# A decoder layer with routed experts: the experts' second layer from the 25th block on as f32r products of high and low parts

## The chip, the cores and the metric

One core of a Trainium2 chip runs the whole program. The metric is the device time of one execution in microseconds, from the hardware. Lower is better. The traces come from one profiled execution.

## The reference

Input x is 4 x 1024 x 256 in f32, a context is 4 x 77 x 256. Three stages follow, each on a layer norm of x and added to x:

```python
x = x + self_attention(layernorm(x))        # 16 heads of 16, a bias that falls with distance
x = x + cross_attention(layernorm(x), ctx)
x = x + ffn(layernorm(x))

def ffn(x):                                  # 8 experts, the best 2 per token
    logits = flat_x @ W_router + b_router
    top_vals, top_idx = top_k(logits, 2)
    router_weights = softmax(logits of the two, -inf elsewhere)
    for e in range(8):
        h = relu(flat_x @ W1[e] + b1[e])     # 256 -> 1024
        y = h @ W2[e] + b2[e]                # 1024 -> 256
        out += y * router_weights[:, e]
```

## The kernel before, in words

The kernel has two phases. In the first, some 1120 us, it computes the attention of four batches. Beside it, the tokens of finished batches are layer-normed and routed, and each token's row (256 values, its number, a code of its expert and two weights) is scattered by GpSimd into a DRAM array `expert_rows` that has one region for each expert.

The second phase goes through 71 blocks (`NBLK`) of 128 rows, all of one expert each. A small table, computed on the chip, says which expert (`expert_of`) and which rows (`row_of`) a block has; it is made in two parts, for blocks below `EARLY` = 40 before the last batch is done and for the others after. The order of all steps on all engines is written out by one planner, `plan()`: it appends steps to one list, with estimated costs in `TAKES`, and each engine later goes through the whole list and does its own kinds of step in that order. Semaphores tie the engines together. `blocks()` (L450) emits for block n:

- `load` (SP): weights of the first layer of block n+3, 1 MB, into one of three buffers `w1_now`; then the block's 128 rows, 130 KB, into one of `NX` = 4 buffers `xi`. SP waits at L990 for the first layer of block n (which frees the buffer of weights), and at L994 for the landed scatter-add of the block that used the same `xi`.
- `up` (TensorE, L1231): first layer of block n+1, in two halves of four chunks of 128 hidden columns, each chunk two f32 products with the rows as the moving side (128 columns). The output is transposed, with hidden units on the partitions. ScalarE (`hid_fore`, L1378) and VectorE (`hid_aft`, L1654) add the bias, take the positive part and write `hidT`, two buffers.
- `xi_turn` (TensorE, L1219) and `xi_turned` (ScalarE, L1364): two transposes of the rows of block n+2.
- `down` (TensorE, L1254): second layer of block n. Eight f32 products add into one PSUM bank; each has a chunk of `hidT` as the stationary side and 256 columns of `w2` as the moving side. All of W2 (8 MB) has been in SBUF since the end of attention; the expert's number is read into a register of TensorE's queue (L1248) first. From block 40 on two banks alternate.
- `yo` (VectorE, L1664 to L1669): the weight of each row from its code, two small chained operations, the bias times this weight, and the sum times the weight out of PSUM into `yo`, two buffers. It waits for the landed scatter-add of block n-2.
- `added` (GpSimd, L1753): an indirect DMA that adds the 128 rows of `yo` into the output in DRAM. L1752 makes it wait until the scatter-add of block n-1 has landed, since two could touch one token.

In the trace an f32 product on TensorE shows as two records, each with its own weight load; so `up` has 32 records for each block and `down` 16.

## Time and profile before

| what | us |
|---|---|
| median of 3 runs (lowest, highest) | 1685.94 (1683.2, 1687.22) |
| the profiled execution's own time | 1687.17 |
| its span, first to last instruction | 1685.3 |
| TensorE busy (matmul) | 1616.5 (96%) |
| VectorE busy | 1026.2 (61%) |
| ScalarE busy | 786.4 (47%) |
| GpSimd busy | 321.8 (19%) |
| mean granted clock of TensorE | 0.986 of full speed |

"Busy" of TensorE is modelled: its records overlap, so that the time from the start of one to the start of the next is what counts, not the duration of one. Idle time of an engine is told with what ended it ("<-"); a wait for several semaphores is put down to one of them. "SPq", "DVEq" or "POOLq" is an engine's instruction queue. The expert phase begins at about 1116 us of the span.

### The profile page before, as it was taken

How to read it: one execution, taken by the hardware profiler on the slowest of the kernel's cores; microseconds unless marked ns; L12 is line 12 of the kernel's file. 1: busy time of each engine (PE TensorE's matmuls, PEld its weight loads, DVE VectorE, ACT ScalarE, POOL GpSimd, SP SyncE). 2: the span in 40 equal slices, each digit the busy share in tenths (PEclk: the TensorE clock that was granted, in tenths of full speed). 3: DMA queues.
4: the chain of work that ended last, by engine and by line, in shares of the span. 5: the costliest groups of instructions: out<-in, count | busy, mean ns of one | idle time of the engine just before them, and what ended most of it. 6: DMA issues, size and time to landing. Idle time of an engine off the chain costs nothing.

```text
span 1685.3 us, 29721 instructions
## 1 busy us (share of the span) xinstructions
PE 1616.5 (96%) x10022; PEld 964.5 (57%) x10022; DVE 1026.2 (61%) x2366; ACT 786.4 (47%) x1635; POOL 321.8 (19%) x310
## 2 busy tenths in 40 slices
PE   5999999999999999999999999989999999999996
PEld 2333334344454444444434453369998899899996
DVE  4888887888777778877788775333444233323322
ACT  3046655666546766655675657742221122121221
POOL 6101120001200041210031100332252222122121
PEclk9789999999999999999999999999999999999998
DMA  6820440333241440323422612235566665656653
GB/s 172 155 70 29 101 80 9 34 42 55 50 70 35 73 80 8 42 60 83 67 56 39 141 49 104 111 107 161 152 199 188 188 188 164 182 168 180 185 163 74
DMA packets 92661, 173.30 MB, mean 103 GB/s; under 512 B 13236, under 2 KB 51124, under 8 KB 92385
## 3 DMA queue, kind: packets, MB, share of 16 engines
q1 hardware_dynamic: 75376, 143.69, 34.0%
q0 software_dynamic: 15744, 26.54, 7.4%
q8 instruction: 82, 1.34, 0.4%
q10 hardware_dynamic: 1392, 1.18, 0.3%
q14 instruction: 67, 0.54, 0.1%
HBM read 133.69 MB, written 37.29 MB: 101 GB/s over the span
## 4 chain that ended last, share of the span: by engine, by line
PE 88%; DVE 3%; ACT 3%; DMA 3%; issue 2%; ACTq 0%; POOL 0%; SPq 0%; POOLq 0%; DVEq 0%
PE ps L1039 15%; PE ps L1254 14%; PE ps L1231 14%; PE ps L1065 14%; PE ps L1025 13%; PE ps L1095 3%; DVE rmax L1409 2%; ACT prob L1272 2%; PE ps L1117 2%; PE ps L1104 2%; PE ps L1151 2%; PE ps L1086 2%; PE ps L1028 2%; PE ps L1068 2%; DMA out<-yo,xi 1%
## 5 line engine op out<-in xcount | busy, mean ns | idle before, releaser
L1409 DVE TENSOR_REDUCE rmax<-ps 128x1 f32<-128x512 f32 x1024 | 665.9, 686 | 198.1 <-PE ps L1065 96.3
L1272 ACT ACTIVATE prob<-ps 128x512 f32<-128x512 f32 x1024 | 560.7, 600 | 331.6 <-PE ps L1028 178.4
L1065 PE MATMUL ps<-stacked_k,stacked_q 112*128 112x512 bf16 x1024 | 397.6, 392 | 10.7 <-DVE rmax L1409 6.3
L1025 PE MATMUL ps<-stacked_q,stacked_k 115*128 115x512 bf16 x1024 | 361.6, 383 | 7.2 <-ACT prob L1272 4.9
L1039 PE MATMUL ps<-prob,values 128*32 128x512 f32 x2048 | 273.5, 606 | 5.6 <-ACT prob L1272 5.6
L1231 PEld LDWEIGHTS ps<-xiT,w_now 128*128 128x128 f32 x2272 | 265.3, 192 | 3.5
L1231 PE MATMUL ps<-xiT,w_now 128*128 128x128 f32 x2272 | 267.1, 275 | 0.0
L1254 PE MATMUL ps<-w,hidT 128*128 x1136 | 259.9, 382 | 6.9 <-issue 5.9
L1065 PEld LDWEIGHTS ps<-stacked_k,stacked_q 112*128 112x128 bf16 x1024 | 100.5, 98 | 285.4 <-DVE rmax L1409 209.9
L1378 ACT ACTIVATE hidT<-ps,b 128x128 f32<-128x128 f32 x284 | 81.1, 368 | 352.8 <-PE ps L1231 315.0
L1254 PEld LDWEIGHTS ps<-w,hidT 128*128 128x128 f32 x1136 | 210.2, 190 | 39.7 <-issue 13.6
L1654 DVE TENSOR_SCALAR hidT<-ps,b 128x128 f32<-128x128 f32 x284 | 80.2, 345 | 201.4 <-PE ps L1231 196.9
L1025 PEld LDWEIGHTS ps<-stacked_q,stacked_k 115*128 115x128 bf16 x1024 | 98.5, 99 | 168.4 <-ACT prob L1272 87.2
L1753 POOL DMA_INDIRECT out<-yo,xi x71 | 111.0, 1563 | 415.4 <-DVE yo L1669 403.2
L1028 PE MATMUL ps<-ramps,slopes 128*128 128x128 f16 x512 | 113.2, 221 | 0.0
L1068 PE MATMUL ps<-ramps,slopes 128*128 128x128 f16 x512 | 113.2, 221 | 0.0
L1669 DVE SCALAR_TENSOR_TENSOR yo<-ps,weight,bias 128x256 f32<-128x256 f32 x71 | 34.3, 484 | 118.8 <-PE ps L1254 118.7
L1739 POOL DMA_INDIRECT expert_rows<-xn,slot x64 | 62.1, 970 | 159.1 <-ACT prob L1272 105.4
L1687 POOL TENSOR_TENSOR rstd_of<-varp,minus_half 128x8 f32<-128x8 f32 (+1 forms) x14 | 21.5, 1533 | 368.6 <-DVE varp L1457 368.6
L1039 PEld LDWEIGHTS ps<-prob,values 128*32 128x32 f32 x2048 | 40.3, 108 | 76.9 <-issue 49.5
L1095 PE MATMUL ps<-xT_next,wqkv 128*128 128x512 f32 x128 | 68.1, 631 | 4.4 <-DVE rest_of L1480 3.2
L1068 PEld LDWEIGHTS ps<-ramps,slopes 128*128 128x128 f16 x512 | 50.5, 99 | 23.1 <-issue 5.4
(181 smaller groups left out, 1128.2 us busy)
## 6 DMA issues: line engine op xcount, KB each, us to landing
w_now<-in_w SPq DMA_DIRECT2D x71, 1024.0 KB
stacked_q<-parts_of_rows SPq DMA_DIRECT2D x90, 128.0 KB, 6.0
stacked_k<-parts_of_rows SPq DMA_DIRECT2D x90, 128.0 KB, 6.6
xi<-expert_rows SPq DMA_DIRECT2D x71, 130.0 KB
w<-in_w SPq DMA_DIRECT2D x8, 1024.0 KB
parts_of_rows<-q_part SPq DMA_DIRECT2D x21, 256.0 KB, 8.7
parts_of_rows<-k_part SPq DMA_DIRECT2D x21, 256.0 KB, 8.8
xr<-in_x POOLq DMA_DIRECT2D x4, 1024.0 KB, 9.6
```

The lines of the kernel that those rows point to most:

```text
L1025: m = e.matmul(ps[:, bank, :], ka[i][0:ROWS, hh, kt * P:(kt + 1) * P], qa[i][0:ROWS, hh, ch * BANK:(ch + 1) * BANK], start=True, stop=True)
L1028: m = e.matmul(ps[:, bank, (kt % 4) * P:(kt % 4 + 1) * P], slopes[:, g * HG + hh, :], ramps[:, kt % 2, :], start=False, stop=True, skip_gr ...
L1039: m = e.matmul(ps[CT * hh:CT * (hh + 1), AV_BANK, :], vt[b % 2][:, kt, c0:c0 + CT], prob[:, unit_of(G, ch, kt, hh) % NPROB, :], start=(kt ...
L1065: m = e.matmul(ps[:, bank, :], qa[i][0:MAX_ROW, hh, qt * P:(qt + 1) * P], ka[i][0:MAX_ROW, hh, kc * BANK:(kc + 1) * BANK], start=True, sto ...
L1068: m = e.matmul(ps[:, bank, (qt % 4) * P:(qt % 4 + 1) * P], slopes[:, g * HG + hh, :], ramps[:, 1 - qt % 2, :], start=False, stop=True, ski ...
L1095: m = e.matmul(ps[:, bank, :], wqkv[:, part, a * D + mo * P:a * D + (mo + 1) * P], xT_next[:, part, ch * BANK:(ch + 1) * BANK], start=firs ...
L1231: m = e.matmul(ps[:, 1 + 2 * (n % 2) + half, q * P:(q + 1) * P], w1_now[n % NW][:, c, f * P:(f + 1) * P], xiT[n % 2][:, c, :], start=(c == ...
L1254: m = e.matmul(ps[:, down_bank(n), 0:D], hidT[n % 2][:, c, :], w2[:, bass.ds(expert, 1), c, :].rearrange("p a f -> p (a f)"), start=(c == ...
L1272: e.activation(prob[:, u % NPROB, :], ps[:, u % NSCORE, :], ACT.Exp).then_inc(sem["exp"], 1)
L1378: m = e.activation(hidT[n % 2][:, q, :], ps[:, 1 + 2 * (n % 2), q * P:(q + 1) * P], ACT.Relu, bias=b1[:, bass.ds(expert, 1), q])
L1409: e.tensor_reduce(rmax[:, G % 2, hh * NT + qt, kc:kc + 1], ps[:, p.bank("max", *k), :], AX.X, ALU.max).then_inc(sem["maxed"], 1)
L1753: e.indirect_dma_start(t["out"], bass.IndirectOffsetOnAxis(ap=xi[n % NX][:, TOKEN:TOKEN + 1].bitcast(I32), axis=0), yo[n % NY][:, :], None ...
```

## The change

From block `FINE` = 24 on, the second layer is computed from two parts of each operand. ScalarE copies the 128x2048 of W2 that the block needs to a high part in the type f32r (`w2_high`), VectorE subtracts it from the original for the low part (`w2_low`), in one instruction, and both keep three buffers. `hidT` is split in the same way in halves (`hid_high` by ScalarE, `hid_low` by VectorE), with two buffers. TensorE then does three f32r products a chunk (high x high, high x low, low x high), 24 a block. Reading the expert's number leaves TensorE's queue for these blocks. Two PSUM banks alternate from block 24 on. The weights of rows move from VectorE to GpSimd for these blocks, as three operations. SP loads a block's rows ahead of its first-layer weights, with five buffers for rows instead of four, in all blocks. An unused tile, `spare`, goes.

```diff
-NX, NY, NW = 4, 2, 3
+NX, NY, NW = 5, 2, 3
+FINE = 24
+NPARTS = 3
@@ plan(), blocks()
+    def split_rows(n, half):
+        add("hid_high", n, half)
+        add("hid_low", n, half)
                 for half in range(2):
                     up_half(n + 1, half)
+                    if n + 1 >= FINE and half == 0:
+                        split_rows(n + 1, 0)
                     yield
             if n + 2 < NBLK:
                 turn_block(n + 2)
+            if FINE <= n + NPARTS - 1 < NBLK and n + 1 > FINE:
+                add("w2_low", n + NPARTS - 1)
+            if FINE <= n + 1 < NBLK:
+                split_rows(n + 1, 1)
+            if n >= FINE:
+                add("yo_weight", n)
             add("down", n)
             add("yo", n)
             add("added", n)
+            if FINE <= n + NPARTS < NBLK:
+                add("w2_high", n + NPARTS)
+                if n + NPARTS < FINE + 2:
+                    add("w2_low", n + NPARTS)
@@ SP
+                    if n >= NX:
+                        e.wait_ge(sem["added"], 16 * (n - NX + 1))
+                    at = e.value_load(row_of[0:1, n:n + 1], ...)
+                    e.dma_start(xi[n % NX][:, :], rows_in[bass.ds(at, P), :]).then_inc(...)
                     if n >= NW:
                         e.wait_ge(sem["up"], p.upto("up", n - NW, 1))
                     if n >= 2:
                         first_layer(n)
-                    (the wait and the rows' DMA stood here)
@@ TensorE
+            def down_in_parts(n, bank):
+                m = n - FINE
+                e.wait_ge(sem["w2_low"], m + 1)
+                for c in range(FC):
+                    if c % (FC // 2) == 0:
+                        e.wait_ge(sem["hid_low"], 2 * m + 1 + c // (FC // 2))
+                    products = ((hid_high, w2_high), (hid_high, w2_low), (hid_low, w2_high))
+                    for i, (rows, weights) in enumerate(products):
+                        last = e.matmul(ps[:, bank, 0:D], rows[n % 2][:, c, :], weights[n % NPARTS][:, c, :],
+                                        start=(c == 0 and i == 0), stop=(c == FC - 1 and i == 2))
+                last.then_inc(sem["down"], 1)
@@ ScalarE
+                elif kind == "hid_high":
+                    e.wait_ge(sem[("hid_fore", "hid_aft")[half]], n + 1)
+                    e.activation(hid_high[n % 2][:, chunks, :], hidT[n % 2][:, chunks, :], ACT.Copy).then_inc(sem["hid_high"], 1)
+                elif kind == "w2_high":
+                    if n >= FINE + NPARTS:
+                        e.wait_ge(sem["down"], n - NPARTS + 1)
+                    expert = e.value_load(expert_of[0:1, n:n + 1], min_val=0, max_val=NE - 1)
+                    e.activation(w2_high[n % NPARTS][:, :, :], second_layer(expert, slice(0, FC)), ACT.Copy).then_inc(...)
@@ VectorE
+                elif kind == "hid_low":
+                    e.wait_ge(sem["hid_high"], p.upto("hid_high", n, half))
+                    if half == 0 and n >= FINE + 2:
+                        e.wait_ge(sem["down"], n - 1)
+                    e.tensor_tensor(hid_low[n % 2][:, chunks, :], hidT[n % 2][:, chunks, :], hid_high[...].bitcast(F32), ALU.subtract)
+                elif kind == "w2_low":
+                    e.wait_ge(sem["w2_high"], p.upto("w2_high", n))
+                    e.tensor_tensor(w2_low[n % NPARTS][:, chunks, :], second_layer(expert, chunks), w2_high[...].bitcast(F32), ALU.subtract)
@@ GpSimd
+                elif kind == "yo_weight":
+                    if n == FINE:
+                        e.wait_ge(sem["yo"], n)
+                    elif n >= FINE + NY:
+                        e.wait_ge(sem["yo"], n - NY + 1)
+                    weigh(e, n, then).then_inc(sem["yo_weight"], 1)
...
```

`weigh` waits for the block's rows and does `is_equal`, `mult`, `add` on 128x1 values, chained by a semaphore. At block 24 ScalarE's first `hid_high` and `w2_high` also wait for all scatters of rows and all stores of attention's output.

## Rows read from the trace of the kernel before

**Rows 1.** Windows: stretch, busy us (count) by engine, clock, DMA share, GB/s.
```profile
1100.00:1150.00 50.00, 45.68 (x312) 37.31 (x309) 15.41 (x55) 20.18 (x48) 17.08 (x20) 1.00 0.40 123
...
1400.00:1450.00 50.00, 49.37 (x340) 46.11 (x339) 15.87 (x55) 10.66 (x35) 10.87 (x7) 1.00 0.63 178
...
1650.00:1690.00 40.00, 22.31 (x137) 19.94 (x135) 8.47 (x28) 3.05 (x10) 6.22 (x4) 0.86 0.25 46
```
**Rows 2.** Chain of waits about one block: start us, us on the chain.
```profile
1406.36 3.57 PE ps L1231 x32
1409.93 0.22 PE ps L1219 x2
1410.15 3.46 PE ps L1254 x16
```
**Rows 3.** All scatter-adds of 1300 to 1660: duration ns min/median/max, first, last start.
```profile
L1753 POOL DMA_INDIRECT out<-yo,xi x48: 1555/1555/1573, 1300.5 to 1655.5; - x48
```
**Rows 4.** Chain of waits in 1324 to 1349, from block 24's scatter-add.
```profile
1331.51 7.41 DMA out<-yo,xi
...
1339.66 6.63 DMA out<-yo,xi
...
1347.04 3.24 DMA xi<-expert_rows
```
**Rows 5.** Waits of SP's queue, 1400 to 1650: total us, times, longest.
```profile
SPq L995 <- DMA out<-yo,xi: 175.1, 33, 6.3
```
**Rows 6.** Timeline of GpSimd, 1482 to 1545: start us, us, [idle before].
```profile
1482.54 1.55 POOL L1753 DMA_INDIRECT out<-yo,xi  x1 [5.45 <-DVE yo L1669]
...
1520.67 1.55 POOL L1753 DMA_INDIRECT out<-yo,xi  x1 [6.08 <-DVE yo L1669]
1528.32 1.56 POOL L1753 DMA_INDIRECT out<-yo,xi  x1 [6.09 <-DVE yo L1669]
1535.98 1.55 POOL L1753 DMA_INDIRECT out<-yo,xi  x1 [6.11 <-DVE yo L1669]
```
**Rows 7.** Timeline of SP's queue in the same stretch.
```profile
1490.40 0.34 SPq L996 DMA_DIRECT2D xi<-expert_rows  x1
...
1521.92 0.24 SPq L865 DMA_DIRECT2D w_now<-in_w  x1
1528.21 0.34 SPq L996 DMA_DIRECT2D xi<-expert_rows  x1
1529.64 0.40 SPq L865 DMA_DIRECT2D w_now<-in_w  x1
1533.29 0.34 SPq L996 DMA_DIRECT2D xi<-expert_rows  x1
...
1541.79 0.34 SPq L996 DMA_DIRECT2D xi<-expert_rows  x1
```
**Rows 8.** Chain of waits in 1655 to 1690, the last two scatter-adds.
```profile
1669.97 3.74 DMA out<-yo,xi
...
1674.46 1.55 POOL out L1753
```
**Rows 9.** Chain of waits in 1436 to 1465, between transposes and second layer.
```profile
1446.77 0.50 issue
```
**Rows 10.** Groups by form, ScalarE and VectorE: busy us, mean ns, idle before.
```profile
L1272 ACT ACTIVATE prob<-ps 128x512 f32<-128x512 f32 x1024 | 560.7, 600 | 331.6 <-PE ps L1028 178.4 <-PE ps L1025 151.9 <-issue 0.6
L1290 ACT ACTIVATE xn<-xr,shift_of,rstd_of 128x256 f32<-128x256 f32 x64 | 37.6, 604 | 0.8 <-DVE shift_of L1463 0.8
L1364 ACT ACTIVATE xiT<-ps 128x256 f32<-128x256 f32 x71 | 27.2, 383 | 59.0 <-PE ps L1219 59.0
...
L1606 DVE TENSOR_TENSOR more_than<-count,steps 128x256 f32<-128x256 f32 x2 | 0.8, 420 | 0.0
L1545 DVE TENSOR_TENSOR chosen<-first,pick_order 128x32 f32<-128x32 f32 x4 | 0.8, 192 | 0.1
```
**Rows 11.** Durations of the bias operation of yo, ns min/median/max.
```profile
L1667 DVE TENSOR_SCALAR bias<-b_all,weight x71: 352/353/611, 1129.5 to 1670.5; 128x256 f32 x71
```

More of the change, by code:

```diff
@@ L79 @@
     "act": {"exp": 0.61, "av": 0.61, "turned": 0.61, "high": 0.7, "norm": 0.55, "cross_exp": 0.9, "p_turned": 0.55, "weigh_exp": 0.35,
-            "c_turned": 0.45, "kv_made": 0.5, "qk_made": 0.5, "cb_made": 0.4, "cv_made": 0.45, "xi_turned": 0.4, "hid_fore": 1.5},
+            "c_turned": 0.45, "kv_made": 0.5, "qk_made": 0.5, "cb_made": 0.4, "cv_made": 0.45, "xi_turned": 0.4, "hid_fore": 1.5,
+            "hid_high": 0.6, "w2_high": 1.95},
     "dve": {"maxed": 0.67, "nmax": 0.3, "nrow": 1.7, "on": 0.75, "stats": 0.42, "aggr": 0.9, "shift": 0.25, "rest": 0.78, "values": 0.9,
             "add1": 0.72, "add2": 0.72, "cross_max": 1.0, "cross_norm": 1.9, "logits_made": 1.8, "second": 1.2, "weigh": 0.2,
-            "chosen": 0.25, "ranked": 2.0, "slots": 1.7, "rows": 1.4, "table": 1.0, "hid_aft": 1.4, "yo": 1.2},
-    "pool": {"rstd": 1.75, "mid": 0.63, "low": 1.2, "bias1": 0.7, "bias2": 0.7, "scatter": 1.3, "added": 1.6, "fetch": 0.9},
+            "chosen": 0.25, "ranked": 2.0, "slots": 1.7, "rows": 1.4, "table": 1.0, "hid_aft": 1.4, "yo": 1.2, "hid_low": 0.65, "w2_low": 2.35},
+    "pool": {"rstd": 1.75, "mid": 0.63, "low": 1.2, "bias1": 0.7, "bias2": 0.7, "scatter": 1.3, "added": 1.6, "fetch": 0.9, "yo_weight": 0.4},
 }
@@ L805, in build @@
             bias = [sb(f"bias{i}", [P, D]) for i in range(NY)]
+            w2_high, w2_low = ([sb(f"w2_{n}{i}", [P, FC, D], F32R) for i in range(NPARTS)] for n in ("high", "low"))
+            hid_high, hid_low = ([sb(f"hid_{n}{i}", [P, FC, P], F32R) for i in range(2)] for n in ("high", "low"))
         flat = lambda ap: ap.rearrange("p a n -> p (a n)")
@@ L1244, in _ @@
                     else:
[L1245 to L1256 removed]
+                        e.wait_ge(sem["yo"], n if n < FINE else n - 1)
+                    if n >= FINE:
+                        down_in_parts(n, down_bank(n))
+                    else:
+                        if n == 0:
+                            e.wait_ge(sem["table"], p.upto("table", 0, TABLE_PARTS - 1))
+                        expert = e.value_load(expert_of[0:1, n:n + 1], min_val=0, max_val=NE - 1)
+                        for c in range(FC):
+                            if c == 0:
+                                e.wait_ge(sem["hid_fore"], n + 1)
+                            elif c == FC // 2:
+                                e.wait_ge(sem["hid_aft"], n + 1)
+                            m = e.matmul(ps[:, down_bank(n), 0:D], hidT[n % 2][:, c, :], w2[:, bass.ds(expert, 1), c, :].rearrange("p a f -> p (a f)"),
+                                         start=(c == 0), stop=(c == FC - 1))
+                        m.then_inc(sem["down"], 1)
         @block.scalar
@@ L1379, in _, with weigh @@
                     m.then_inc(sem["hid_fore"], 1)
+                elif kind == "hid_high":
+                    n, half = k
+                    chunks = slice(half * FC // 2, (half + 1) * FC // 2)
+                    if half == 0 and n == FINE:
+                        e.wait_ge(sem["scattered"], n_scatters(NB - 1))
+                        e.wait_ge(sem["stored"], 16 * (NB + 1))
+                    e.wait_ge(sem[("hid_fore", "hid_aft")[half]], n + 1)
+                    e.activation(hid_high[n % 2][:, chunks, :], hidT[n % 2][:, chunks, :], ACT.Copy).then_inc(sem["hid_high"], 1)
+                elif kind == "w2_high":
+                    n, = k
+                    if n == FINE:
+                        e.wait_ge(sem["scattered"], n_scatters(NB - 1))
+                        e.wait_ge(sem["stored"], 16 * (NB + 1))
+                    elif n == EARLY:
+                        e.wait_ge(sem["table"], p.upto("table", 1, TABLE_PARTS - 1))
+                    if n >= FINE + NPARTS:
+                        e.wait_ge(sem["down"], n - NPARTS + 1)
+                    expert = e.value_load(expert_of[0:1, n:n + 1], min_val=0, max_val=NE - 1)
+                    e.activation(w2_high[n % NPARTS][:, :, :], second_layer(expert, slice(0, FC)), ACT.Copy).then_inc(sem["w2_high"], 1)
+        def weigh(e, n, then):
+            w, x = weight[n % NY], xi[n % NX]
+            e.wait_ge(sem[f"slots_in{n % NX}"], 16 * (n // NX + 1))
+            if n < FINE:
+                then(e.scalar_tensor_tensor(out=w[:, :], in0=x[:, CODE:CODE + 1], scalar=code_of[:, n:n + 1], in1=x[:, MORE:MORE + 1],
+                                            op0=ALU.is_equal, op1=ALU.mult))
+            else:
+                then(e.tensor_scalar(w[:, :], x[:, CODE:CODE + 1], code_of[:, n:n + 1], None, ALU.is_equal))
+                then(e.tensor_tensor(w[:, :], w[:, :], x[:, MORE:MORE + 1], ALU.mult))
+            return e.tensor_tensor(w[:, :], w[:, :], x[:, SECOND:SECOND + 1], ALU.add)
         def split_rest(e, kind, b, mo, a, ch):
@@ L1673, in _, with then @@
         def _(e):
+            links = [0]
+            def then(ins):
+                links[0] += 1
+                ins.then_inc(sem["pool_chain"], 1)
+                e.wait_ge(sem["pool_chain"], links[0])
             for i in range(NSET):
```

51 lines of the change are left out of this document (26 added, 25 removed).

## The prediction

> **What bounds the kernel now.** I read the windows first, then the chain of waits of single blocks, then the queues by time. In the windows of the expert phase TensorE is busy nearly all the time at the full clock, VectorE and ScalarE under a third, and the DMA engines about 0.6 [rows 1]. In the chain a block has 32 records of the first layer and 16 of the second; one that waits for nothing takes 3.57 + 0.22 + 3.46 = 7.25 us of TensorE [rows 2].
>
> The blocks do not run at 7.25. The scatter-adds into the output, one per block, give the beat: 48 of them between 1300.5 and 1655.5, so 355.0 / 47 = 7.55 us [rows 3]. The reader should see in the chain what the missing 0.3 us is: from block 24 on it goes through a scatter-add's DMA of 7.41 us, the next one's 6.63 us, and then SP's read of a block's rows, 3.24 us [rows 4]. Two loops stand behind it.
>
> Loop 1, scatter to scatter: L1752 lets a scatter start only when the one before has landed. From landing (1331.51 + 7.41) to the next start (1339.66) are 0.74 us [rows 4]. SP waits for the same landing before it fetches rows (5.3 us in each of 33 blocks [rows 5]), and issues them at the same offset, so SP's issue at L996 marks the turnaround in the queue's timeline: the scatter of 1482.54 is followed by the issue at 1490.40 (7.86 us), that of 1520.67 by 1528.21 (7.54), that of 1528.32 by 1533.29 (4.97) [rows 6, 7]. Of the eight pairs from 1482.54 to the last, 1535.98 and 1541.79, six lie between 7.33 and 7.86 and two at 4.97 and 5.81; the mean is 6.99. The page books GpSimd's idle time on VectorE's yo; yet in five of the eight the next scatter starts within 0.11 us of SP's issue (1528.21 and 1528.32), so the landing decides it as much as yo does.
>
> Why so long? The 1 MB weight load is issued 1.1 to 1.4 us after the rows, by the same SP wait. When it comes 1.25 us after the scatter (1521.92) the turnaround is 7.54; at 1.32 (1529.64) it is 4.97 [rows 6, 7]; with no load left, the landing takes 3.74 [rows 8]. So the two transfers race, and a few hundredths of a us decide.
>
> Loop 2, the rows' ring of four: landing of scatter k, rows k+4 (3.24 us above), TensorE's transposes, the expert's number read by TensorE's queue, second layer, yo, scatter. It shows as 0.50 us of "issue" ahead of the second layer [rows 9], in most blocks after the 20th.
>
> **The change, part by part.** *Products.* Per block 16 records at 3.46 / 16 = 0.216 us go, 24 f32r products of 256 columns come. No row shows f32r. Bounds: a record with four-byte weights and 256 column-passes paces at 3.57 / 32 = 0.112, and a transpose, 128 columns with such weights, at 0.22 / 2 = 0.11 [rows 2]: half the columns save nothing, so the weight load alone seems to cost about that, and less is not in sight. The other end is 0.216, the record of the old layer. I take 0.112, the nearest row where 256 columns pass once: 24 x 0.112 = 2.69, and the block's TensorE work is 3.79 + 2.69 = 6.48, against 7.25. The ends are 6.4 and 8.97.
>
> By the Trainium skill (FP8 and Floating Point Precision, TensorE Precision Notes) true f32 takes four passes and the reduced form is read once and cut to 22 bits; by that the sum would be the 6.48 above. No trace here shows it.
>
> *ScalarE.* Per block it gains two copies of 128x512 and one of 128x2048, all from SBUF. Slope from PSUM rows: (600 - 383) / 256 = 0.85 ns an element; 128x256 from SBUF takes 604 [rows 10]. So 0.60 to 0.82 each and 1.9 to 2.13. By the same slope hid_fore's four pieces of 128x128 are 1.1; with the 0.38 of xi_turned it works 4.6 to 5.3 of a block. *VectorE.* From 128x256 in 420 ns and 128x32 in 192 [rows 10]: 1.02 ns an element, so 0.69 twice and 2.27, and hid_aft's four pieces are 1.2; with yo and its bias (about 0.4 each) about 5.7 a block.
>
> These sit on a loop: w2_high(n+3) waits for down(n), because of three buffers, and hid_fore(n+2) is queued behind it. After down(n): value_load and copy 2.9, hid_fore 1.2, hid_high 0.75, hid_low 0.7, hid_aft 1.15, w2_low 2.3, hid_low 0.75, down(n+2) 2.75: 12.5 for two blocks, or 6.3 to 6.6 each. About TensorE's own 6.48; it costs nothing as long as the beat is above that.
>
> *Weights of rows on GpSimd.* Three 128x1 operations a block, put between two scatters, where GpSimd is idle 5.4 us and more [rows 6]. Their result is due 4 us later. Zero; if the cover went, up to 1.5 us.
>
> *Rows ahead of weights, ring of five.* SP's cycle keeps its order (wait, rows, weights), so the race of loop 1 stays. Loop 2 gets one block more and stops binding: from landing k to scatter k+3 are 0.75, the rows' 3.2, VectorE's hid_aft, w2_low, hid_low and yo 5.1, a hop of 0.3, and some 6.7 to land: 16 over three blocks, 5.4 each. The read of the expert's number goes from TensorE's queue.
>
> *What is late next.* Loop 1 alone, which no edit touches. TensorE at 6.5 runs ahead until a load of rows or weights stops it, which SP issues behind the landings, at the same beat. Then yo is always early and every scatter starts 0.74 after the landing before it. Taking the mixture of before, between the 6.99 of the eight pairs and the 7.52 of the six slow ones, I set 7.20 a block.
>
> **The sum.** Blocks 24 to 67: scatters at 1331.51 [rows 4] and 1655.5 [rows 3], 43 steps of 7.53; 43 x 0.33 = 14. The last three steps, 19.0 us to 1674.46 [rows 8]: with no load beside them, three of 3.74 + 0.74 make 13.4, so 5.6. Blocks 16 to 24 without loop 2: about 2. Attention, some two thirds of the span, is untouched. Together 22 us from the profiled 1687.2: 1665. The median of the runs shown is 1.2 lower, which I leave in the range.
>
> TensorE will idle some 0.7 us in each block. The clock should hold: in 1100 to 1150 it idled 4.3 of 50 us at 1.00, and fell to 0.86 only where it idled 18 of 40 [rows 1].
>
> **Rivals.** *TensorE becomes the bound again:* the race at 1.25 against 1.32 us tips to the short turnaround, 5 us, and the block runs at 6.5. 43 x 1.03 + 5.6 + 2 = 52, so 1635. For it: a few hundredths decide, and other code stands around them. Against: only a quarter of the turns were won, and with a shorter block the load comes nearer the scatter.
>
> *The race is always lost:* 7.52 a block, 43 x 0.01 + 5.6 + 2 = 8, so 1679.
>
> *f32r paces like the old record,* 0.216: the block takes 8.97 and the kernel 43 x 1.44 + about 3 = 65 more, 1752. It decides from (7.53 - 3.79) / 24 = 0.156 us a product. For it: the operands are four bytes, as in the record that paces at 0.216. Against: that record passes its columns twice.
>
> *VectorE holds GpSimd.* The last bias operation takes 611 ns instead of 353, beside a scatter's preparation on GpSimd, 1669.97 to 1671.52 [rows 8, 11]: they share something. w2_low would hold the preparation by up to 2.3 us where they meet, inside loop 1. Met in every third block, that is 0.7 a block: 7.9, so 43 x 0.37 = 16 less the 8 of the other steps, 1695; met always, far more. It decides from 0.5 us a block. Against: the 48 scatters took 1.555 to 1.573 [rows 3].
>
> The Trainium skill (GPSIMD Engine Reference, Specifications) says that GpSimd's SBUF interfaces are shared with VectorE, with contention from instructions with two SBUF inputs, which w2_low and hid_low are and the old block's bulk was not; the 611 ns agree that there is contention.
>
> **How the numbers follow.** Forecast 0.45, own range 1655 to 1676; TensorE bound, or on the way there, 0.2; race lost 0.13; f32r slow 0.09; VectorE in the way 0.08; nothing measurable 0.05. A measurement of this kernel tells 0.2% (3.4 us) from no change. Faster 0.77, same 0.08, slower 0.15. The range from 1638 to 1690 leaves out 0.1 at each end.
>
> **What would show it.** L1254's successor with 24 records a block at about 0.11 us; the second layer in 2.7 us; no "issue" ahead of it; scatters 7.2 us apart with SP's rows issued at the same time as each; VectorE over 70% busy. A beat of 6.5 would mean the race was won. A beat above 7.6 would make me wrong: then either the products pace over 0.156 or the scatter's preparation is longer than 1.55.

## The result: slower by 0.3%, and outside the forecast range

The kernel after takes 1691.88 us (median of 20 runs, 1684.26 to 1705.3), the kernel before beside it 1687.29 us (20 runs, 1683.2 to 1691.08). The ratio is 1.0029, 95% interval [1.0018, 1.004]. The profiled execution of after took 1695.34 us, with a span of 1693.5 us and a mean clock of 0.982. That is 8 us more than the profiled 1687.2 us of before; 1665 us were forecast.

### The profile page after: what moved, and what is told of

Read it like the earlier page. It is cut to its first block, busy times and chain, and to the rows that moved or that the text cites. A ratio compares the mean times of both kernels' runs of the same rounds, so it can differ in the third digit from the quotient of the medians.

```text
span 1693.5 us, 30735 instructions
## 1 busy us (share of the span) xinstructions
PE 1594.4 (94%) x10398; PEld 960.5 (57%) x10398; DVE 1169.1 (69%) x2413; ACT 932.8 (55%) x1776; POOL 381.1 (23%) x451
## 4 chain that ended last, share of the span: by engine, by line
PE 69%; DMA 21%; DVE 3%; issue 3%; ACT 3%; ACTq 0%; POOL 0%; SPq 0%; POOLq 0%; DVEq 0%
DMA out<-yo,xi 20%; PE ps L1080 15%; PE ps L1106 14%; PE ps L1066 13%; PE ps L1272 5%; PE ps L1298 4%; PE ps L1136 3%; DVE rmax L1486 2%; ACT prob L1316 2%; PE ps L1158 2%; PE ps L1145 2%; PE ps L1192 2%; PE ps L1109 2%; PE ps L1127 2%; PE ps L1069 2%
## 5 line engine op out<-in xcount | busy, mean ns | idle before, releaser
L1272 PE MATMUL ps<-xiT,w_now 128*128 128x128 f32 x2272 | 271.5, 277 | 32.8 <-issue 32.8
L1864 POOL DMA_INDIRECT out<-yo,xi x71 | 128.8, 1813 | 356.9 <-DMA out<-yo,xi 244.3
L1432 ACT ACTIVATE hid_high<-hidT 128x512 fp32r<-128x512 f32 x94 | 59.3, 631 | 96.0 <-DVE hidT L1731 94.5
L1037 PE MATMUL ps<-w_high,hid_high 128*128 128x256 f32 x376 | 110.1, 293 | 0.0
L1748 DVE TENSOR_TENSOR w_low<-w,w_high 128x2048 fp32r<-128x2048 f32 x47 | 107.8, 2293 | 2.4 <-issue 1.9
L1037 PE MATMUL ps<-w_low,hid_high 128*128 128x256 f32 x376 | 106.2, 283 | 0.0
L1037 PE MATMUL ps<-w_high,hid_low 128*128 128x256 f32 x376 | 106.1, 282 | 0.0
L1444 ACT ACTIVATE w_high<-w 128x2048 fp32r x47 | 89.9, 1912 | 22.0 <-PE ps L1037 12.9
```

The costliest lines, as they stand in the source:

```text
L1037: last = e.matmul(ps[:, bank, 0:D], rows[n % 2][:, c, :], weights[n % NPARTS][:, c, :], start=(c == 0 and i == 0), stop=(c == FC - 1 and i ...
L1272: m = e.matmul(ps[:, 1 + 2 * (n % 2) + half, q * P:(q + 1) * P], w1_now[n % NW][:, c, f * P:(f + 1) * P], xiT[n % 2][:, c, :], start=(c == ...
L1444: e.activation(w2_high[n % NPARTS][:, :, :], second_layer(expert, slice(0, FC)), ACT.Copy).then_inc(sem["w2_high"], 1)
L1748: e.tensor_tensor(w2_low[n % NPARTS][:, chunks, :], second_layer(expert, chunks), w2_high[n % NPARTS][:, chunks, :].bitcast(F32), ALU.subt ...
L1864: e.indirect_dma_start(t["out"], bass.IndirectOffsetOnAxis(ap=xi[n % NX][:, TOKEN:TOKEN + 1].bitcast(I32), axis=0), yo[n % NY][:, :], None ...
```

## The profile after, read against the rows of before

From the page of after: the scatter-add's group and the groups of the new second layer (busy us, mean ns of one, idle time ahead and what ended it).

```profile
L1864 POOL DMA_INDIRECT out<-yo,xi x71 | 128.8, 1813 | 356.9 <-DMA out<-yo,xi 244.3
L1432 ACT ACTIVATE hid_high<-hidT 128x512 fp32r<-128x512 f32 x94 | 59.3, 631 | 96.0 <-DVE hidT L1731 94.5
L1037 PE MATMUL ps<-w_high,hid_high 128*128 128x256 f32 x376 | 110.1, 293 | 0.0
```

The groups by form hold the rest.

```profile
L1748 DVE TENSOR_TENSOR w_low<-w,w_high 128x2048 fp32r<-128x2048 f32 x47 | 107.8, 2293 | 2.4 <-issue 1.9
L1444 ACT ACTIVATE w_high<-w 128x2048 fp32r x47 | 89.9, 1912 | 22.0 <-PE ps L1037 12.9 <-issue 9.0
L1740 DVE TENSOR_TENSOR hid_low<-hidT,hid_high 128x512 fp32r<-128x512 f32 x94 | 64.4, 685 | 10.0 <-ACT hid_high L1432 9.7
L1760 DVE TENSOR_SCALAR bias<-b_all,weight 128x256 f32 x71 | 25.2, 354 | 104.2 <-POOL weight L1456 100.1 <-DVE weight L1456 4.1
```

The work of each engine is what the forecast said: 2293 ns for 2.27, 685 for 0.69, 1912 for 1.9 to 2.13, 631 for 0.60 to 0.82. One row is not: the scatter-add's record on GpSimd, its preparation, takes 1813 ns in the mean, where before every one took 1555 to 1573 [rows 3]. This is all scatters of 1300 to 1660 in after, with their duration (min/median/max, first and last start) and the time from the start to the landing of the data.

```profile
L1864 POOL DMA_INDIRECT out<-yo,xi x46: 1553/1797/3065, 1299.0 to 1653.2; - x46
...
DMA to landing us min/median/max: 4.3/7.0/8.4
```

They come every 354.2 / 45 = 7.87 us, against 7.55 [rows 3]. The windows of after answer to [rows 1].

```profile
1100.00:1150.00 50.00, 45.67 (x311) 37.12 (x308) 15.55 (x56) 20.39 (x48) 17.28 (x20) 1.00 0.43 133
1400.00:1450.00 50.00, 43.57 (x367) 42.37 (x365) 36.39 (x62) 28.93 (x50) 14.78 (x24) 1.00 0.63 180
```

TensorE is busy 43.57 of 50 us, where before it was 49.37, at the same full clock; VectorE went from 15.87 to 36.39. TensorE has the time that its shorter block gives, and spends it waiting. The chain of waits, where before it went through both loops [rows 4], is now one loop only.

```profile
1498.36 7.08 DMA out<-yo,xi
1505.44 0.03 issue
1505.46 0.02 POOLq L1863
1505.48 0.50 issue
1505.98 0.02 POOLq L1449
1506.00 0.19 issue
1506.19 7.28 DMA out<-yo,xi
...
1514.23 6.91 DMA out<-yo,xi
```

Landing, 0.75 us, scatter, landing: loop 1 of the forecast. A scatter starts within 0.8 us of the landing before it in 40 of the 42 steps between blocks 24 and 66; in before it did in 15. The waits of the stretch 1400 to 1650 say the same (total us, times, longest): GpSimd waits for the landing 31 times, where before the page booked its idle time on yo.

```profile
POOL out L1864 <- DMA out<-yo,xi: 152.7, 31, 6.5
DVE bias L1760 <- POOL weight L1456: 74.0, 33, 3.9
```

So the step that failed is inside this loop. The timelines of VectorE and of GpSimd in one stretch (start us, us, idle before) show a first part of it.

```profile
1456.45 2.29 DVE L1748 TENSOR_TENSOR w_low<-w,w_high 128x2048 fp32r<-128x2048 f32 x1
...
1464.61 2.29 DVE L1748 TENSOR_TENSOR w_low<-w,w_high 128x2048 fp32r<-128x2048 f32 x1
...
1471.91 2.29 DVE L1748 TENSOR_TENSOR w_low<-w,w_high 128x2048 fp32r<-128x2048 f32 x1
```

```profile
1458.47 1.76 POOL L1864 DMA_INDIRECT out<-yo,xi  x1 [5.00 <-DMA out<-yo,xi]
1459.71 0.87 POOL L1454 TENSOR_SCALAR weight<-xi,code_of 128x1 f32<-128x1 f32 x1
...
1466.29 2.08 POOL L1864 DMA_INDIRECT out<-yo,xi  x1 [5.17 <-DMA out<-yo,xi]
...
1473.80 1.88 POOL L1864 DMA_INDIRECT out<-yo,xi  x1 [4.54 <-DMA out<-yo,xi]
```

Add the end of each w_low and 1.47 us: 1458.74 + 1.47 = 1460.21, and the scatter's preparation ends at 1460.23; 1466.90 gives 1468.37, it ends at 1468.37; 1474.20 gives 1475.67, it ends at 1475.68. The preparation is held by the w_low that runs when it starts, and ends 1.47 us behind it. hid_low holds it in the same way. From block 24 on, 31 of 47 preparations are longer than 1.65 us, up to 3065 ns, and each ends 1.46 to 1.50 us behind such an instruction: 17 behind a w_low, 14 behind a hid_low. The mean is 1.90 us. That is 0.35 us a block, while the landing became later by 1.0 us (mean of blocks 24 to 65: 7.09 against 6.10). The rest has to be found by experiments.

Where the 8 us are, from the scatters' starts in the two traces: up to block 24, 1.1 less; blocks 24 to 67, 338.3 us against 324.0, 14.2 more; the last three steps, 14.2 against 18.9, 4.7 less.

## The experiments

Theory A: VectorE's instructions with two inputs from on-chip memory hold the scatter's preparation. Theory B: the race of scatter and weight load alone, tipped by moved timing. Theory C, formed later: GpSimd's own small instructions behind a scatter hold it. All runs are summed up here; times are medians, ratios are to the kernel before, run beside each. Beat (scatter to scatter) and landing (start to landing) are means over the 42 steps between blocks 24 and 66, preparation over blocks 24 to 70, all of the one profiled execution, so they can differ from the median's tendency: kernels bound by the landing vary by 3 to 21 us from run to run.

| kernel | us | ratio, 95% interval | beat | landing | preparation |
|---|---|---|---|---|---|
| before | 1687.29 | 1 | 7.53 | 6.10 | 1.56 |
| after | 1691.88 | 1.0029 [1.0018, 1.004] | 7.87 | 7.09 | 1.90 |
| ring_alone | 1673.33 | 0.9903 [0.9875, 0.9931] | 7.24 | 6.45 | 1.56 |
| no_w2_low | 1685.3 | 0.9964 [0.9944, 0.9983] | 7.76 | 6.98 | 1.64 |
| two_outputs | 1643.09 | 0.9721 [0.9704, 0.9738] | 6.69 | 5.45 | 1.65 |
| load_behind_prep | 1646.49 | 0.9734 [0.9713, 0.9755] | 6.62 | 4.51 | 1.69 |
| weights_on_dve | 1681.84 | 0.9984 [0.9967, 1.0001] | 7.38 | 6.60 | 2.04 |
| low_behind_prep | 1688.37 | 1.0029 [1.0011, 1.0048] | 7.76 | 6.81 | 1.63 |
| ring_two_input | 1688.35 | 1.003 [1.0018, 1.0041] | 7.60 | 6.81 | 2.89 |
| ring_one_input | 1674.28 | 0.9944 [0.9927, 0.9961] | 7.32 | 6.53 | 1.56 |
| ring_gpsimd_weights | 1675.62 | 0.995 [0.9932, 0.9969] | 7.43 | 6.65 | 1.60 |
| no_w2_low_weights_on_dve | 1679.44 | 0.9967 [0.995, 0.9985] | 7.39 | 6.53 | 1.57 |
| gate_all | 1642.32 | 0.9754 [0.9734, 0.9773] | 6.68 | 3.98 | 1.68 |
| gate_all_f32 | 1668.76 | 0.9911 [0.9892, 0.9929] | 7.24 | 3.83 | 1.57 |
| products_alone | 1671.65 | 0.9909 [0.9891, 0.9927] | 7.42 | 6.64 | 1.56 |
| splits_alone | 1682.56 | 0.9972 [0.9955, 0.999] | 7.67 | 6.89 | 2.08 |
| products_w2_high | 1678.95 | 0.9953 [0.9939, 0.9968] | 7.50 | 6.72 | 1.56 |
| products_hid_split | 1676.41 | 0.9942 [0.9926, 0.9958] | 7.38 | 6.60 | 1.59 |

### First four: which part, and which loop

**ring_alone**: the kernel before with the two queue edits.

```diff
-NX, NY, NW = 4, 2, 3
+NX, NY, NW = 5, 2, 3
 (and SP issues a block's rows ahead of its weight load, as in the change)
```

> The kernel before with only the order of SP's loads and the ring of five rows' buffers changed. Theory A (the scatter-add's preparation on GpSimd is held by VectorE's two-input instructions; nothing of that is here): preparation stays 1.555 us, the 'issue' ahead of the second layer goes, the beat falls from 7.53 to 7.2 to 7.5 us a block, 1668 to 1682 us. Theory B (once every scatter-add starts right behind the landing before it, it loses the race with the weight load each time, without any help of VectorE): the beat is 7.5 to 7.8 and the time 1683 or more.

Measured 0.9903: B in its form "1683 or more" is refuted, A holds so far. Still 37 of the 42 landings take over 6 us. The two edits alone gain 16 us. All edits that were meant to speed the products up make it 21 us worse (1.0029 - 0.9903 = 0.0126).

**no_w2_low**: after, the low part of W2 left out; the second product reads the high part.

```diff
-e.tensor_tensor(w2_low[...], second_layer(expert, chunks), w2_high[...].bitcast(F32), ALU.subtract)
-products = ((hid_high, w2_high), (hid_high, w2_low), (hid_low, w2_high))
+products = ((hid_high, w2_high), (hid_high, w2_high), (hid_low, w2_high))
```

> The changed kernel without VectorE's w2_low; the product that read it reads w2_high again, so TensorE's work is the same (the low part of W2 is left out of the result). Theory A: most preparations fall from 1.8 us to 1.56 to 1.65, a few held by hid_low up to 2.1, more races are won, beat 7.2 to 7.5 instead of 7.8, 1668 to 1680 us. Theory B: the beat stays at 7.7 to 7.9, 1688 to 1695 us.

Half of the loss comes back (0.0065), less than A gave and more than B: the preparation is nearly short again (1.64) and the landing still takes 6.98 us. There is a second cause.

**two_outputs**: after, odd blocks are added to a second array, so that a scatter waits for the last but one. The final sum of the two arrays is left out, and each batch is stored twice.

```diff
-e.wait_ge(sem["added"], 16 * n)
-e.indirect_dma_start(t["out"], ...)
+e.wait_ge(sem[f"added{n % 2}"], 16 * (n // 2))
+e.indirect_dma_start((t["out"], out2)[n % 2], ...)
```

> The changed kernel, with the scatter-adds of odd blocks going to a second array in DRAM, so that each waits for the landing of the one before the last (the final sum of the two arrays is left out, and each finished batch is stored twice). Both theories: the serial wait is the only bound, so the beat falls to that of TensorE or of the ScalarE-VectorE loop, 6.6 to 6.9 us, and the time to 1640 to 1655 us. If another loop (weights, rows) binds close behind, the beat stays above 7.3 and the time above 1670.

**load_behind_prep**: after; from block 28 on, SP holds each weight load until GpSimd has the scatter beside it prepared, and issues it ahead of the rows.

```diff
+if n >= FINE + 4:
+    e.wait_ge(sem["up"], p.upto("up", n - NW, 1))
+    e.wait_ge(sem["yo_weight"], n - 4 - FINE + 1)
+    first_layer(n)
```

> The changed kernel, with SP's load of first-layer weights from block 28 on ahead of the rows, and waiting for GpSimd's yo_weight of block n-4, which is queued behind the scatter-add of block n-5, instead of following that scatter-add's landing. Both theories: the load comes after the preparation, the race is always won, landings fall from 7.0 to 3.8 to 4.5 us, the beat to 6.6 to 6.9, the time to 1638 to 1652 us. If the landings stay near 7 us, the weight load beside them was not what makes them long; time 1685 or more.

Both take the chain of landings apart, each in its own way, and both come to the TensorE-bound beat: 6.6 to 6.7 us. In load_behind_prep the race is mostly won: 29 of 42 landings take under 5 us, and TensorE never idles in this window.

```profile
1400.00:1450.00 50.00, 50.00 (x438) 50.00 (x438) 41.77 (x68) 33.80 (x58) 21.03 (x29) 1.00 0.67 189
```

The traces also tell what decides the race. The prediction compared the starts of the load's issue, 1.25 and 1.32 us behind the scatter. The ends are farther apart, and they lie on two sides of the end of the scatter's preparation [rows 6, 7]. The issue of 1521.92 ends at 1522.16, 0.06 us before the preparation does (1520.67 + 1.55 = 1522.22), and the race is lost; that of 1529.64 ends at 1530.04, 0.16 us after it (1528.32 + 1.56 = 1529.88), and the race is won. It is so throughout, between blocks 24 and 66 of the fourteen traces in which nothing holds the load (two_outputs left aside), wherever a load is issued beside a scatter. Where the issue ended before the preparation or less than 0.1 us after it, none of 530 landings took under 5 us. Where it ended later, 45 of 48 did. In ring_alone it ends 0.08 us too early in the median. A longer preparation can thus turn a won race into a lost one, and one edit does little more than that (ring_two_input, below).

### Second four: the preparation

**weights_on_dve**: after, the rows' weights made by VectorE again (two instructions ahead of the bias, as in before).

```diff
-if n < FINE:
-    then(weigh(e, n, then))
-else:
-    e.wait_ge(sem["yo_weight"], n - FINE + 1)
+then(weigh(e, n, then))
```

> The changed kernel, with the weights of rows back on VectorE. So far: ring_alone beats at 7.28 us a block with preparations of 1.556 us, the changed kernel at 7.80 with 1.90, and its scatter-adds' first packets come 5.5 us after their start instead of 4.2. Theory A1 (VectorE's work of a block is released by GpSimd's weights, which stand behind the scatter-add, takes 5.7 us and so ends in w2_low or hid_low just where GpSimd prepares the next one): the preparations fall to 1.56 to 1.65 us in most blocks, beat 7.2 to 7.4, 1667 to 1676 us. Theory A2 (VectorE's two-input work is in the way wherever it stands): preparations 1.8 or more, time 1686 or more. Theory C (GpSimd's own operations behind the scatter-add delay its descriptors, no_w2_low's 4.45 us): first packets at 4.2 us instead of 4.45 to 5.5.

**low_behind_prep**: after; w2_low waits until the scatter beside it is prepared.

```diff
+if n - 2 >= FINE:
+    e.wait_ge(sem["yo_weight"], n - 2 - FINE + 1)
 e.tensor_tensor(w2_low ...
```

> The changed kernel, with w2_low waiting for yo_weight, that is until the preparation of the scatter-add ahead of it is over. Theory A1: VectorE's order stays the same and so does the release, so w2_low moves little; the preparations stay at 1.75 to 1.95 us, the time within 5 us of 1690. Theory A2: w2_low now never meets a preparation, those of 2.6 to 3.1 us go, the mean falls under 1.8 and the time by 3 to 10 us.

Neither came out by any of the theories. weights_on_dve has longer preparations than after, 2.04, and is faster, 0.9984; low_behind_prep has them at 1.63 and gains nothing, 1.0029.

**ring_two_input** and **ring_one_input**: ring_alone with one unused VectorE instruction of 2.29 us right behind each landing.

```diff
+e.tensor_tensor(extra[:, :, :], w2[:, 0, :, :], w2[:, 1, :, :], ALU.subtract)   # two_input
+e.tensor_reduce(extra[:, :, 0], w2[:, 0, :, :], AX.X, ALU.max)                  # one_input
```

> ring_alone (the kernel before with the new order of loads and five rows' buffers) with one more VectorE instruction a block from the 25th, which subtracts one 128x2048 f32 tile from another in SBUF, ahead of yo and right behind the landing that the next scatter-add waits for as well. The sum is used for nothing. Theory A: GpSimd's preparation is held until it ends, 1.55 -> 2.5 to 3.0 us, the race is always lost, beat 7.28 -> 7.6 to 8.3, 1685 to 1715 us. Theory B (no tie between VectorE and the preparation): 1.556 us and 1670 to 1677 us as in ring_alone.

> The same place, with a reduction over one 128x2048 f32 tile in SBUF instead, about as long (2.2 to 2.3 us) but with one input. Theory A in the form that two inputs matter: preparations 1.555 us, beat 7.2 to 7.4, 1668 to 1678 us. If any VectorE work on SBUF holds GpSimd: as ring_two_input.

This pair is the proof of A. The timelines of ring_two_input, first VectorE, then GpSimd:

```profile
1448.55 2.29 DVE L1665 TENSOR_TENSOR extra<-w 128x2048 f32<-128x2048 f32 x1 [2.56 <-DMA out<-yo,xi]
...
1451.32 0.55 DVE L1669 TENSOR_SCALAR bias<-b_all,weight 128x256 f32 x1 [0.15 <-DVE weight L1668]
...
1456.20 2.29 DVE L1665 TENSOR_TENSOR extra<-w 128x2048 f32<-128x2048 f32 x1 [2.32 <-DMA out<-yo,xi]
```

```profile
1449.23 3.04 POOL L1755 DMA_INDIRECT out<-yo,xi  x1 [4.92 <-DMA out<-yo,xi]
1456.86 3.07 POOL L1755 DMA_INDIRECT out<-yo,xi  x1 [4.59 <-DMA out<-yo,xi]
```

And ring_one_input, the same two engines:

```profile
1455.96 2.29 DVE L1665 TENSOR_REDUCE extra<-w 128x8 f32<-128x2048 f32 x1
...
1463.58 2.29 DVE L1665 TENSOR_REDUCE extra<-w 128x8 f32<-128x2048 f32 x1 [0.37 <-DMA out<-yo,xi]
```

```profile
1455.73 1.56 POOL L1755 DMA_INDIRECT out<-yo,xi  x1 [5.96 <-DMA out<-yo,xi]
1464.16 1.56 POOL L1755 DMA_INDIRECT out<-yo,xi  x1 [6.87 <-DMA out<-yo,xi]
```

Same length, same place in the queue. With two inputs the preparation ends 1.4 us behind the VectorE instruction (1450.84, 1452.27), in 42 of the 43 blocks in which that runs when the scatter starts. With one it takes its 1.56 right through it, in all 23 such blocks; the second pair of lines is one. The pair differs in the output too, 128x2048 against 128x8. Writing alone holds nothing in what these traces have, which is shorter instructions: in ring_alone eight `hidT` and seven `bias` operations, which write 128x128 and 128x256 values to on-chip memory, run on for 0.19 to 0.34 us past a scatter's start, and its preparation still takes 1.56 to 1.57.

The two-input instruction costs 14 us over the other (1688.35 against 1674.28), and it does so by the race alone: no short landing is left (0 of 42 under 5 us, against 4), while the long ones take 6.81 us in the mean as against 6.80, though they are prepared 1.3 us later. Against ring_alone, run at another time, the one-input instruction may itself cost up to some us (0.9944 against 0.9903, intervals overlapping).

The Trainium skill (SBUF — State Buffer, Who interferes with whom) infers that tensor_tensor, which takes only the read interface shared with GpSimd, does not stall descriptor generation. This pair shows that it does stall that of a scatter-add with an index tile, by 1.5 us a piece; on tensor_reduce, which by the page never contends, the two agree.

But A is not the whole: low_behind_prep has the preparation repaired and gains nothing, and weights_on_dve, with a longer one, is 0.0045 faster than after. What weights_on_dve takes away is GpSimd's three instructions behind each scatter: hence theory C.

### Third four: GpSimd's own instructions, and the way out

**ring_gpsimd_weights**: ring_alone, the rows' weights on GpSimd from block 24 on.

```diff
-then(e.scalar_tensor_tensor(out=w[:, :], in0=x[:, CODE:CODE + 1], ...))   # VectorE
+weigh on GpSimd, three instructions behind scatter n - 1, then yo waits for yo_weight
```

> The kernel before with the two queue edits (rows ahead of the weight load, five buffers for rows) and, as in the kernel after, the rows' weights on GpSimd from block 24 on, in the three short instructions that stand behind each scatter in GpSimd's queue. No f32r product, no low or high parts. The same kernel without the GpSimd weights took 1673 us (beat 7.17 and 7.28 us a block, landings of 6.4 to 6.5 us, first packets of a scatter 4.2 us behind its start). Theory C (GpSimd's own instructions behind a scatter hold back the scatter's packets, whoever the other engine is): landings of 6.9 us, a beat of 7.6 to 7.7, 1683 to 1690 us. Theory A (only VectorE's instructions with two inputs from memory hold the preparation): 1670 to 1677 us, beat as without them. Between: each has a share.

C has a share: 0.995 against 0.9903 is 8 us (the intervals, from two comparisons at different times, just do not overlap). The time in us, 1675.62, lies in A's range, so the ratio alone is thin. The traces add that the lost races get longer: the median landing of over 5 us is 6.95 to 7.10 us in the four kernels that have these instructions and no held load (after, no_w2_low, low_behind_prep, ring_gpsimd_weights), and 6.67 to 6.81 in the nine changed kernels that do not. The preparation is 1.60 instead of 1.555.

```profile
L1779 POOL DMA_INDIRECT out<-yo,xi x45: 1587/1604/1622, 1335.9 to 1658.8; - x45
...
DMA to landing us min/median/max: 3.7/6.9/8.2
```

**no_w2_low_weights_on_dve**: after with both causes away, the two diffs above together (the low part of W2 is left out again).

> The kernel after without the low part of W2 (the third product reads the high part in its place, so what is computed differs and TensorE's work is the same) and with the rows' weights back on VectorE. Left out alone, the low part gave 1685 us; the weights moved back alone gave 1682 us with a beat of 7.35 and 7.40. Theory A and C together: both causes are gone, landings of 6.3 to 6.5 us, beat 7.1 to 7.25, 1668 to 1675 us. Theory A alone: as with the low part left out alone, 1685 us. Theory C alone: as with the weights moved back alone, 1682 us.

Not as expected: 0.9967, no better than either alone. The two are not additive, and something else holds 11 us (0.9967 against the 0.9903 of ring_alone).

**gate_all**: after, with the weight load held from block 5 on, by a mark of GpSimd.

```diff
 e.indirect_dma_start(t["out"], ..., compute_op=ALU.add).then_inc(sem["added"], 16)
+e.memset(mark[:, n:n + 1], 0.0).then_inc(sem["prepared"], 1)
...
+if n >= NX:
+    e.wait_ge(sem["up"], p.upto("up", n - NW, 1))
+    e.wait_ge(sem["prepared"], n - 4)
+    first_layer(n)
```

> The kernel after, with each weight load from block 5 on held back behind the preparation of the scatter that it has raced with so far: a 1-column memset of GpSimd behind every scatter counts up a semaphore, and SP's load for block n waits for that of block n - 5 and stands ahead of the rows' load. The same from block 28 on took 1646.5 us, with landings of 4.3 us and TensorE always busy. Race theory: the blocks 5 to 24 (19 blocks) now fall from a beat of 7.87 to TensorE's own 7.25, 8 to 12 us less: 1634 to 1640 us. If the early blocks are bound by something else: 1644 to 1648 us, their beat unchanged.

**gate_all_f32**: the same two edits on ring_alone, the second layer in f32.

> The kernel before with five buffers for rows and the same held-back weight load from block 5 on, the second layer in f32 throughout: no part of the f32r edit. It tells what that edit is worth once the landing is no bound. TensorE's own beat of 7.25 us in f32 would bind all blocks: against 1673 us for the queue edits alone, only the 19 early blocks gain, 8 to 12 us: 1661 to 1667 us, TensorE busy all the time. The difference from the f32r kernel with the same load order is then 24 to 29 us, which is 43 blocks of 0.6 us.

gate_all is steady (1641.37 to 1643.69 in 5 runs) and about as fast as load_behind_prep (0.9754 against 0.9734, intervals overlapping). The gain forecast for blocks 5 to 24 is not there: their beat is 7.80, with landings of 3.99. TensorE itself binds them: in its trace it is busy all of 1180 to 1325, and the chain of waits there is TensorE alone, with some 9 us for the last batch's tokens (L1210, L1133 and others) between the blocks of 7.25. gate_all_f32, at 1668.76, is just above its expected range too. The timelines show how the race is avoided: GpSimd first, then SP's queue.

```profile
1508.10 1.59 POOL L1870 DMA_INDIRECT out<-yo,xi  x1 [1.31 <-DVE yo L1768]
1509.16 0.65 POOL L1872 MEMSET mark<- 128x1 f32 x1
```

```profile
1506.21 0.34 SPq L1026 DMA_DIRECT2D xi<-expert_rows  x1
1510.61 0.39 SPq L894 DMA_DIRECT2D w_now<-in_w  x1
```

The load's issue starts 2.51 us behind the scatter instead of 1.1 to 1.3, and ends 1.3 us behind its preparation in the median. The scatter's packets leave 2.2 us behind its start in the mean and it lands after 3.9 us; in after they leave 5.0 us behind it, behind the load's 1 MB. Scatters of gate_all, then of gate_all_f32:

```profile
L1870 POOL DMA_INDIRECT out<-yo,xi x46: 1586/1603/2034, 1334.7 to 1630.5; - x46
...
DMA to landing us min/median/max: 3.5/3.9/5.3
```

```profile
L1758 POOL DMA_INDIRECT out<-yo,xi x46: 1567/1567/1586, 1333.8 to 1656.9; - x46
...
DMA to landing us min/median/max: 3.6/3.8/5.3
```

With equal landings only TensorE's block differs. The chains of gate_all and then of gate_all_f32:

```profile
1404.26 3.57 PE ps L1278 x32
1407.84 0.22 PE ps L1266 x2
1408.05 2.88 PE ps L1043 x24
```

```profile
1506.80 3.57 PE ps L1236 x32
1510.37 0.22 PE ps L1224 x2
1510.59 3.46 PE ps L1259 x16
```

6.67 against 7.25 us. The f32r edit is then worth 1668.76 - 1642.32 = 26 us, which is its 43 blocks of 0.6. It was never slow; it had no path to the end.

### Last four: what holds the rest

**products_alone**: weights_on_dve with the parts made once; the 24 products of each block stay, all later copies and differences go (the result differs).

```diff
+if n >= FINE + 2:         # in hid_high and hid_low
+    continue
+if n >= FINE + NPARTS:    # in w2_high and w2_low
+    continue
```

> The kernel after with the rows' weights on VectorE, and without the splitting from block 27 on: the parts of W2 and of the hidden rows are made for the first blocks alone and used again, so that the 24 f32r products of a block stay and all copies and differences of ScalarE and VectorE go (the result differs). What is open: with the low part of W2 left out and the weights moved back together the kernel still took 1679 us, where the queue edits alone took 1673. If the shorter TensorE block is what costs (it moves the weight load in the race): 1677 to 1682 us, a beat of 7.35 to 7.45. If the rest of the splitting costs (the copies of ScalarE, the differences of the hidden rows): 1668 to 1675 us, a beat of 7.15 to 7.28, as with the queue edits alone.

**splits_alone**: weights_on_dve with all copies and differences, waited for as before, and 16 f32 records of the second layer.

```diff
-rows[n % 2][:, c, :], weights[n % NPARTS][:, c, :]
+hidT[n % 2][:, c, :], w2[:, bass.ds(expert, 1), c, :]
```

> The counterpart: the kernel after with the rows' weights on VectorE and all the splitting of ScalarE and VectorE, waited for as before, but the second layer multiplied from the f32 operands in 16 records a block; the TensorE block is the old 7.25 us. If the splitting costs by itself: the same 1682 us as with the weights moved back (which has the f32r products too), a beat of 7.35 to 7.5. If the cost comes from the shorter TensorE block: 1670 to 1676 us, apart from the preparations that w2_low holds. With VectorE's 5.7 us a block below the beat either way, its load alone binds nothing.

The two stand apart: products alone 0.9909, as the queue edits alone; splitting alone 0.9972, as weights_on_dve. The shorter TensorE block costs nothing, the splitting costs the rest.

**products_w2_high** and **products_hid_split**: products_alone with ScalarE's copy of W2 back in each block, or with the splitting of the hidden rows back.

```diff
-if n >= FINE + NPARTS:    # in w2_high alone
-    continue
-if n >= FINE + 2:         # in hid_high and hid_low alone
-    continue
```

> The kernel with the f32r products alone (1671.65 us, 0.9909 of the kernel before), and with ScalarE's copy of W2, 128x2048 and 1.9 us, in every block again. Nothing else of the splitting. If that copy is what the rest costs (ScalarE reads and writes 1 MB of on-chip memory beside the scatter and its landing): 0.996 to 0.998 of the kernel before, 1678 to 1682 us. If not: 0.989 to 0.993.

> The same kernel of the f32r products alone, with the splitting of the hidden rows instead: ScalarE's two copies of 128x512 and VectorE's two differences of 690 ns in every block; the parts of W2 are made for the first blocks alone. If the hidden rows' splitting costs the rest (its differences have two inputs from memory and lie between the scatters; it also delays the second layer by their time): 0.996 to 0.998. If the copy of W2 does: 0.989 to 0.993. If both are near 0.994 the cost is shared.

Each has a share: 0.0044 and 0.0033 over products_alone, 7 and 6 us; the first interval, [0.9939, 0.9968], is above that of products_alone, the second, [0.9926, 0.9958], just overlaps it. The preparation is not held in the first (1.56) and hardly in the second (1.59). So the copy of ScalarE costs in another way than A. Which way is open: the landings of its profiled run are 0.08 us longer in the mean, but that run, at 1676.32 us, is its fastest, and the one of products_alone, at 1679.08, its slowest. Not by lost races: 4 and 5 landings of 42 take under 5 us, against 3 in products_alone.

## Why the prediction was wrong, step by step

**Products: right in kind, off by 0.19 us a block.** The f32r product was to pace at 0.112 us and the block to take 6.48; 24 take 2.88, so 0.120 each, and the block 6.67. The rival at 0.216 is out.

**ScalarE and VectorE: the durations were right**, within 0.03 us on VectorE (the slope of [rows 10] gives 2.25 for w_low where the prediction writes 2.27; it takes 2.29), and their loop of 6.3 to 6.6 us does not bind: gate_all runs at 6.68 with it.

**Rows first, ring of five: right.** Loop 2 is gone from the chain. Blocks 16 to 24: 1.7 us gained, 2 forecast. The last three steps: 4.7 gained, 5.6 forecast.

**What failed: "Loop 1 alone, which no edit touches", at 7.20 a block.** That loop 1 would be the bound was right, and without the splitting its size was near: ring_alone gives 7.24 (with TensorE's old 7.25 beside it as a second bound) and products_alone, where TensorE needs only 6.67, 7.42, at 0.9909 of before, 15 us gained. The false part is that no edit touches it: 7.87 was measured, so that of 43 steps with 14 us to gain came 14 us lost. Edits touch it in four ways, each added alone to a kernel without it: a two-input instruction behind each landing (14 us, the worst placing), the rows' weights on GpSimd (8), ScalarE's copy of W2 (7), the splitting of the hidden rows (6). The last two have no mechanism shown, and the last one's interval just overlaps that of products_alone. The sum, 35, is above the 21 that after loses to ring_alone, so they do not add.

In the two traces the loss comes in two ways. Of ring_alone's 5 short landings after keeps 1: 4 x 2.5 = 10 us. Its long landings take 7.16 us in the mean against 6.75: 41 x 0.41 = 17 us. Together that is the 27 us by which the two profiled executions differ in these blocks. The first is what a held preparation does, by ring_two_input; the second goes with GpSimd's instructions, by the medians above, and in part stays open. The prediction took the mixture of short and long landings over from before, as if it were a property of the loop; it follows from a margin of a tenth of a us, which edits move.

**"Weights of rows on GpSimd ... Zero" failed too.** The cover of 5.4 us was there, and the wait of VectorE for the result (74 us in 33 blocks) is off the chain; but the instructions stand right behind the scatter in the queue, where its preparation and packets are still under way.

**The rival "VectorE holds GpSimd" named the first mechanism, at 0.08.** It gave 1695 us; the profiled execution took 1695.34 and the median is 1691.88. That it comes so near is luck. Its mechanism is confirmed by ring_two_input; its price was not: met in more blocks than assumed (31 of 47, not a third, 14 of them by hid_low) but shorter (0.35 us a block, not 0.7), costing nothing in a race that is lost anyway, and the rest of the loss came from elsewhere. The argument against it, that the 48 scatters of before took 1.555 to 1.573, was empty: before, VectorE had no long two-input instruction in a block to hold them with.

**"TensorE becomes the bound again", at 1635,** was right on what a won race is worth: gate_all, 1642, wins 41 of 42. The forecast treated the race as luck, to be drawn; it was one wait away from being set.

## What to carry to other kernels

When scatter-adds form a serial chain, price every edit by what it does between a scatter's start and its landing: here a VectorE instruction with two on-chip inputs lengthened the preparation, GpSimd's next instructions the landing, and a large load issued before the preparation ended put 2.5 us on it. Where a time comes in two sizes, find what decides between them before forecasting with the mean. Before making an engine faster, take the transfer that binds off the critical loop: here one wait that sends the weight load behind the scatter's preparation turned a loss of 5 us into a gain of 42. A row whose duration never varies proves nothing about a load that it has not yet met.

## What the runs showed of the hardware

- GpSimd's preparation of a scatter-add of 128 rows takes 1.555 us. It is held by a two-input VectorE instruction running at its start and then ends 1.4 to 1.5 us behind it (ring_two_input, after); a one-input instruction of the same 2.29 us holds nothing (ring_one_input). It works the other way too: in ring_two_input the bias operation beside the preparation takes 0.55 us instead of 0.35.
- A scatter beside a 1 MB load lands around 4.1 us after its start when the load's issue ends over 0.1 us behind the preparation (45 of 48 under 5 us), and around 6.7 us in ring_alone, 7.0 in after, when it ends earlier (0 of 530 under 5 us). In ring_alone its first packets leave at 2.1 or at 4.1 us. With the issue started 2.5 us behind it, it lands after 3.9 us in the median (gate_all).
- Three 128x1 instructions of GpSimd right behind a scatter go with a preparation of 1.60 instead of 1.555 us and long landings of 6.95 us in the median instead of 6.72 (ring_gpsimd_weights, ring_alone).
- Kernels whose landings race spread by 3 to 21 us over their runs, gate_all by 2.3.
- An f32r product of 256 columns and 128x128 weights paces at 0.120 us (24 in 2.88, gate_all). In f32 it is two records of 0.216, so 0.43 (16 in 3.46, gate_all_f32). Three f32r products for one in f32, 0.36 against 0.43, are what the edit gains.
